# Input stage of a delta-rule layer: scans, decay projection, gathers, beta and averages in another order

## The chip, the cores and the metric

The kernel is one program on one core of a Trainium2 chip. Its engines work from queues of their own: TensorE (PE, matrix products and transposes), VectorE (DVE), ScalarE (ACT), GpSimd (POOL) and SyncE (SP, which issues transfers). They wait for one another through semaphores. The metric is the device time in microseconds (us) of the whole program.

## The reference, cut to what matters

Two layers run over 4096 tokens of width 256: causal linear attention and a mixture of eight experts (top two), then the delta-rule layer and a recurrent output stage. The change lies in the input part of the delta-rule layer. What it must compute:

```python
def short_conv(x, w):                 # 4 taps over the tokens
    ...
q = silu(short_conv(hidden_states @ Wq, conv_q))
k = silu(short_conv(hidden_states @ Wk, conv_k))
v = silu(short_conv(hidden_states @ Wv, conv_v))
mix_inp = silu(short_conv(hidden_states @ Wmix, conv_mix))
q = silu(q)
k = silu(k)
beta = jax.nn.sigmoid(hidden_states @ Wb)
gamma = jax.nn.sigmoid(hidden_states @ Wdec)
# ema_rule, for each head:
s = gt[..., None] * s + (1.0 - gt[..., None]) * vt
# delta rule: q and k to unit length, then k_beta @ k^T in chunks of 32, strictly lower part, its inverse
mix = jax.nn.sigmoid(mix_inp + mix_bias)
```

`hidden_states` is the layer-normed residual, to which the two chosen experts' rows have just been added.

## The kernel before

`build` calls `first_layer` (attention and experts), `delta_inputs` (the change is in it alone), `delta_rule` and `gated_output`. Between them all engines meet, so what `delta_inputs` gives up at its end moves all that follows.

`delta_inputs` works on eight groups (`NG`) of 512 tokens, features on the partitions. Every engine runs the same software pipeline of ten steps: in step i it handles group i (`new`: expert rows added, statistics, normed `xn`), group u = i - 1 (`here`: projections, convolutions, scans) and group v = i - 2 (`tiles`: transposes to token rows, Gram matrices, norms). Nothing reorders work: each engine's queue is what `step` writes.

- **Projections (PE `use(n)`, ACT `use(n)`).** `use(0)` and `use(1)` transpose `xn` into `xT`. The other nine follow `ORDER`: 4 and 5 are the two 128-row blocks of v, 2 and 3 of k, 0 and 1 of q, `"s"` is the small rows (beta, decay, mix with their taps), and `"g0"`, `"g1"` spread the decay row over the partitions, which needs `"s"` copied out first (four copies, line 1334). Three PSUM banks `pp` go round: a product may start when ScalarE has emptied the bank of three before. A block takes two ScalarE copies (lines 1343 and 1346).
- **Convolutions (DVE `conv(b)`).** Three multiply-adds at line 1479 on each block, then ScalarE's `silu(b)`: once for 4 and 5, twice for the others. The silus of 0 and 1 stand in ScalarE's next step.
- **Average (scans).** ScalarE puts tanh of g0 and g1 in `dec_t` (line 1339); GpSimd rescales it to `dec` (line 1294); VectorE makes the input (line 1515) and runs two scans (line 1521) that carry on from the previous group. `rows(...)`, in steps 5 to 8 only, computes rows of the first inverses (lines 1094 and 1097); SyncE sends them (line 1082) in step 9.
- **Token rows (PE, ACT `tokens(n)`).** Six transposes in two PSUM banks: n = 0, 3 of k, 1, 4 of v, 2, 5 of the averages. SyncE stores a pair of tiles after its three.
- **Norms.** ScalarE squares, PE `sums()` adds them up (line 1627), VectorE adds epsilon (`ss`, line 1529), forms scales and `l32` (line 1541), GpSimd takes powers (`root`, line 1301). Beta and mix come from `small_rows()` through ScalarE's tanh and silu; line 1498 (`sm_m`) feeds the second tanh (line 1413), which feeds lines 1508 and 1509.
- **GpSimd** besides gathers the expert rows of group i + 1 (line 1258, eight transfers, in two lots of four), and makes `rstd` (line 1283).

## Time and profile before

| | |
|---|---|
| time, median of 3 runs (lowest, highest) | 1425.54 us (1422.87, 1429.32) |
| the profiled execution: its time, its span | 1430.96 us, 1429.3 us |
| busy: PE, DVE, ACT, POOL | 89%, 58%, 32%, 35% of the span |
| `delta_inputs`, from its first gather to the next stage's start | 610 to 913 us |
| steps 2 to 4 of it (VectorE's) | 663.37 to 759.80 us |
| steps 5 to 7 | 759.80 to 856.06 us |
| mean granted TensorE clock | 0.919 |

The profiled execution is 5.4 us (0.4%) above the median of the runs; changes are summed against its rows and then taken off either. A row of a timeline reads: start, length, engine, line, operation, output <- inputs, shapes, count, and in brackets how long the engine stood idle before it and what released it. "PEclk" is the share of TensorE's full clock that was granted.

### The profile page before, as it was taken

The numbers are of one execution on the slowest core, as the hardware profiler recorded it, in microseconds if no ns is written. First come the engines' busy times: TensorE is split into PE (matmuls) and PEld (weight loads), VectorE is DVE, ScalarE is ACT, GpSimd is POOL, SyncE is SP. The second block draws the span as 40 slices with busy tenths as digits, with TensorE's granted clock in tenths as the row PEclk, the third lists the DMA queues.
The fourth block names the chain that finished last, engine by engine and source line by source line (L and its number), as shares of the span: only waits on it lengthen the run. The fifth ranks groups of instructions, "written<-read, shape, count | busy, mean of one in ns | idle before, by whom it ended". The sixth has DMA issues, their size and how long they took to land. (4 is left out here: it accounts for less than half of the span.)

```text
span 1429.3 us, 36337 instructions
## 1 busy us (share of the span) xinstructions
PE 1274.9 (89%) x12853; PEld 951.0 (67%) x12854; DVE 822.0 (58%) x1882; ACT 463.4 (32%) x1085; POOL 497.4 (35%) x711
## 2 busy tenths in 40 slices
PE   6999999899999999927889787498999999889997
PEld 5888888767777777614555454387888888646564
DVE  5778888633222222238789887357566666435443
ACT  1211112132222222217667776112222222123332
POOL 3334666414511111064665642223343444210000
PEclk9999999989999999968878888559999999779999
DMA  9999910112321111121454433712643335000001
GB/s 313 351 369 341 330 44 35 36 51 100 118 64 59 59 59 59 52 77 52 141 142 128 123 89 94 195 50 74 111 108 95 95 94 149 7 1 30 30 22 37
DMA packets 219962, 156.60 MB, mean 110 GB/s; under 512 B 111744, under 2 KB 201344, under 8 KB 219840
## 3 DMA queue, kind: packets, MB, share of 16 engines
q1 hardware_dynamic: 210528, 129.51, 30.9%
q0 software_dynamic: 9312, 25.44, 5.3%
q8 instruction: 80, 1.31, 0.4%
q14 instruction: 42, 0.34, 0.1%
HBM read 64.47 MB, written 90.44 MB: 108 GB/s over the span
## 5 line engine op out<-in xcount | busy, mean ns | idle before, releaser
L945 PE MATMUL ps_sc<-w,a_qeo 128*128 x568 | 183.3, 466 | 0.0
L753 DVE TENSOR_TENSOR a_stm<-a_vpad,ps_sc 128x352 f32<-128x352 f32 x71 | 37.0, 521 | 177.3 <-ACT a_vpad L517 156.6
L945 PEld LDWEIGHTS ps_sc<-w,a_qeo 128*128 128x128 f32 x568 | 104.1, 193 | 46.5 <-issue 2.5
L423 POOL DMA_DIRECT2D x_slots<-a_stm x66 | 36.5, 552 | 226.1 <-issue 226.1
L1583 PE MATMUL d_pp<-d_xT,d_w_p 128*128 128x512 f32 x192 | 110.3, 721 | 1.1 <-ACT d_xT L1328 1.1
L1479 DVE SCALAR_TENSOR_TENSOR d_cout<-d_cin,d_taps,d_cout 128x512 f32<-128x512 f32 x144 | 106.2, 747 | 6.4 <-ACT d_cout L1346 3.0
L915 PE MATMUL ps_kv<-w,a_stm 128*128 x426 | 105.7, 384 | 1.2 <-DVE a_stm L746 1.2
L915 PEld LDWEIGHTS ps_kv<-w,a_stm 128*128 128x128 f32 x426 | 79.3, 190 | 30.2 <-issue 12.7
L2326 PE MATMUL g_pp<-g_xT,g_w_g 128*128 128x512 f32 x192 | 89.3, 604 | 8.3 <-ACT g_xT L2217 8.3
L1258 POOL DMA_INDIRECT got<-x_slots,d_idx x64 | 74.0, 1156 | 18.7 <-issue 16.1
L517 ACT ACTIVATE a_vpad<-ps_sc 128x352 f32<-128x352 f32 x71 | 33.0, 464 | 140.1 <-PE ps_sc L945 140.1
L711 DVE TENSOR_TENSOR a_stm<-ps_sc,causal 128x2048 f32<-128x2048 f32 x32 | 73.0, 2282 | 1.7 <-PE ps_sc L854 1.3
L1583 PEld LDWEIGHTS d_pp<-d_xT,d_w_p 128*128 128x128 f32 x192 | 41.7, 232 | 45.8 <-issue 41.7
L415 POOL DMA_INDIRECT x_slots<-xn_res,slots x64 | 65.3, 1020 | 15.1 <-issue 14.8
L746 DVE COPY a_stm<-ps_t 128x384 f32<-128x384 f32 x71 | 39.6, 557 | 47.7 <-PE ps_t L924 47.4
L1824 POOL TENSOR_SCALAR u_ms<-u_ss 128x4 f32<-128x4 f32 x32 | 6.2, 195 | 173.1 <-DVE u_ss L1936 173.1
L890 PE MATMUL ps_qk<-a_xnT,w_qk 128*128 128x128 f32 x512 | 66.1, 283 | 0.0
L2326 PEld LDWEIGHTS g_pp<-g_xT,g_w_g 128*128 128x128 f32 x192 | 36.5, 193 | 44.2 <-issue 32.9
L890 PEld LDWEIGHTS ps_qk<-a_xnT,w_qk 128*128 128x128 f32 x512 | 61.3, 196 | 0.0
L2260 DVE TENSOR_TENSOR g_z<-g_py,g_b_o 128x256 f32<-128x256 f32 x32 | 13.6, 425 | 77.0 <-PE g_py L2341 77.0
L2063 PE MATMUL u_bank_g<-u_qkT 64*128 64x128 f32 x512 | 41.8, 308 | 17.3 <-DMA u_kve<-rec 17.3
L1876 ACT ACTIVATE u_GU<-u_bank_g 64x256 f32<-64x256 f32 x32 | 12.1, 378 | 134.9 <-PE u_bank_g L2063 134.9
(275 smaller groups left out, 2839.8 us busy)
## 6 DMA issues: line engine op xcount, KB each, us to landing
x_slots<-a_zeros SPq DMA_DIRECT2D x32, 1024.0 KB, 10.9
rec<-d_kve SPq DMA_DIRECT2D x32, 384.0 KB, 2.9
u_kve<-rec SPq DMA_DIRECT2D x32, 384.0 KB, 3.5
a_qeo<-x_slots SPq DMA_DIRECT2D x71, 128.0 KB
x_slots<-a_stm POOLq DMA_DIRECT2D x66, 128.0 KB
rec<-d_act_out SPq DMA_DIRECT2D x32, 256.0 KB
u_qkT<-rec SPq DMA_DIRECT2D x32, 256.0 KB, 3.1
w<-in_w SPq DMA_DIRECT2D x4, 1408.0 KB, 13.9
```

What stands on the lines that cost most here:

```text
L415: pool.indirect_dma_start(out=x_slots, out_offset=bass.IndirectOffsetOnAxis(ap=slots[:, choice, t:t + 1], axis=0), in_=xn2_res[:, t, :], i ...
L711: dve.tensor_tensor(stm[:, :, :], ps_sc[:, :].rearrange("p (h q) -> p h q", h=16), causal[:, :].unsqueeze(1).broadcast_to([P, 16, P]), ALU ...
L746: dve.tensor_copy(e_hT[:, q], ps_h[:, 0:3 * P].rearrange("p (b t) -> p b t", b=3)).then_inc(ht_out, 1)
L753: dve.tensor_tensor(e_h[:, q, 0:HID], e_gate[:, q, :], ps_3[q], ALU.mult).then_inc(h_out, 1)
L890: mm = pe.matmul(ps_qk[:, b * P:(b + 1) * P], w_qk[:, k, b * P:(b + 1) * P], xnT[:, q, k, :], start=(k == 0), stop=(k == KD - 1))
L915: mm = pe.matmul(ps_y, e_hT[:, q, b, :], w2[:, b, bass.ds(e_out, 1), :], start=(b == 0), stop=(b == 2))
L945: mm = pe.matmul(ps, e_xT[:, q, k, :], w13[:, s, k, bass.ds(e_hidden, 1), :], start=(k == 0), stop=(k == KD - 1))
L1258: pool.indirect_dma_start(out=got[:, q, j, s, :], out_offset=None, in_=x_slots, in_offset=bass.IndirectOffsetOnAxis(ap=idx[:, q, s, j:j + ...
L1479: dve.scalar_tensor_tensor(out=cout[:, b, :], in0=x[:, c:c + GW], scalar=taps[:, b, c:c + 1], in1=cout[:, b, :], op0=ALU.mult, op1=ALU.add)\
L1583: mm = pe.matmul(bank[:, :], lhs, xT[:, k, :], start=(k == 0), stop=(k == KD - 1))
L2063: mm = pe.matmul(b_g[:, e, z, n, :], qkT[rows, gs, 2 + n, :], qkT[rows, gs, what + n, :], start=True, stop=True)
L2326: mm = pe.matmul(bank[:, :], w_g[:, k, b // 2, (b % 2) * P:(b % 2 + 1) * P], xT[:, q, k, :], start=(k == 0), stop=(k == KD - 1))
```

## The change

Only orders change; every operation and its size stay.

- VectorE: the decay input and the two scans (with `rows`, where there are any) go from between mix and block 2's convolution to the end of the step. The three beta instructions go from behind block 5's convolution to ahead of block 4's (the fourth block, counted from 0). The convolution of block 3 moves ahead of the norms' scales.
- `ORDER` becomes 4, 5, 2, 3, "s", 0, 1, "g0", "g1".
- `tokens` run in the order 0, 1, 3, 4, 2, 5 (`TOK`): both averages last. TensorE's `sums()` moves ahead of `"s"`. SyncE waits accordingly and stores both pairs later.
- GpSimd: the second lot of gathers goes ahead of the rescale to `dec`, and that rescale also behind `root` and its two copies.
- ScalarE: `silu(2)` and `silu(3)` go between the last three `use`s, `silu(4)` ahead of `"s"`.

VectorE, one steady step before, from the end of block 5's convolution on (`d_ema` rows are the two scans, `d_cout` rows the convolutions, `d_l` is `l32`):

```order
L1496 TENSOR_SCALAR d_beta<-d_sm_t 128x16
L1497 TENSOR_SCALAR d_beta<-d_sm_t 128x16
L1498 TENSOR_TENSOR d_sm_m<-d_sm_m,d_mix_b 128x16
L1504 TENSOR_SCALAR d_xn<-x_res,d_mom,d_rstd 128x256 x4
L1508 TENSOR_SCALAR d_rest<-d_sm_t 128x16
L1509 TENSOR_SCALAR small<-d_sm_t 128x4x4
L1515 SCALAR_TENSOR_TENSOR d_dec_t<-d_dec_t,d_act_out 128x1024
L1521 SCALAR_TENSOR_TENSOR d_ema<-d_dec,d_ema,d_dec_t 128x512 x2
L1479 SCALAR_TENSOR_TENSOR d_cout<-d_cin,d_taps,d_cout 128x512 x3
L1529 TENSOR_SCALAR d_ss<-d_ps_s 128x32
```

The same stretch now:

```order
L1509 TENSOR_SCALAR d_xn<-x_res,d_mom,d_rstd 128x256 x4
L1513 TENSOR_SCALAR d_rest<-d_sm_t 128x16
L1514 TENSOR_SCALAR small<-d_sm_t 128x4x4
L1484 SCALAR_TENSOR_TENSOR d_cout<-d_cin,d_taps,d_cout 128x512 x6
L1521 TENSOR_SCALAR d_ss<-d_ps_s 128x32
L1524 RECIPROCAL d_over<-d_ss 128x16
L1527 TENSOR_TENSOR small<-d_beta,d_over 128x4x4
L1528 TENSOR_TENSOR small<-d_beta,d_over 128x4x4
L1533 TENSOR_TENSOR d_l<-d_ps_g,small 128x8x32 x2
L1484 SCALAR_TENSOR_TENSOR d_cout<-d_cin,d_taps,d_cout 128x512 x6
L1544 SCALAR_TENSOR_TENSOR d_dec_t<-d_dec_t,d_act_out 128x1024
L1550 SCALAR_TENSOR_TENSOR d_ema<-d_dec,d_ema,d_dec_t 128x512 x2
```

The scans moved past four convolutions and the scales; the beta rows have gone ahead of this stretch.

GpSimd, one steady step before:

```order
L1254 COPY d_idx<-slots 128x8
L1258 DMA got<-x_slots,d_idx 128x256 x4
L1281 TENSOR_SCALAR d_shifted<-d_mom 128x4
L1283 TENSOR_TENSOR d_rstd<-d_shifted,d_power 128x4
L1294 TENSOR_SCALAR d_dec<-d_dec_t 128x1024
L1258 DMA got<-x_slots,d_idx 128x256 x4
L1301 TENSOR_TENSOR d_root<-d_ss,d_power 128x32
```

and now:

```order
L1283 TENSOR_SCALAR d_shifted<-d_mom 128x4
L1285 TENSOR_TENSOR d_rstd<-d_shifted,d_power 128x4
L1260 DMA got<-x_slots,d_idx 128x256 x4
L1299 TENSOR_TENSOR d_root<-d_ss,d_power 128x32
L1302 TENSOR_TENSOR small<-d_root,d_rest 128x4x4
L1303 COPY small<-d_root 128x4x4
L1307 TENSOR_SCALAR d_dec<-d_dec_t 128x1024
L1311 COPY d_cin<-d_cin 128x6x3
```

The rescale to `d_dec` now stands behind four gathers and the powers.

TensorE, the middle of one steady step now (`d_w_s` is the "s" projection, `d_sel_q` the sums, `d_sel_d` g0 and g1); before, "s" stood ahead of the sums by seven rows:

```order
L1624 MATMUL d_ps_g<-d_act_out 32x32 x64
L1588 MATMUL d_pp<-d_xT,d_w_p 128x512 x2
L1605 MATMUL d_ps_tok<-d_ident,d_act_out 128x128 x4
L1588 MATMUL d_pp<-d_xT,d_w_p 128x512 x2
L1633 MATMUL d_ps_s<-d_sel_q,d_sq 128x8 x16
L1588 MATMUL d_pp<-d_xT,d_w_s 128x512 x2
L1605 MATMUL d_ps_tok<-d_ident,d_ema 128x128 x4
L1588 MATMUL d_pp<-d_xT,d_w_p 128x512 x2
L1605 MATMUL d_ps_tok<-d_ident,d_ema 128x128 x4
L1588 MATMUL d_pp<-d_xT,d_w_p 128x512 x2
L1579 MATMUL d_pp<-d_s_rows,d_sel_d 128x512 x2
```

The averages' transposes, the decay's products and "s" are all late in the step.

The core of the diff:

```diff
-        ORDER = [4, 5, "s", 2, "g0", "g1", 3, 0, 1]
+        ORDER = [4, 5, 2, 3, "s", 0, 1, "g0", "g1"]
...
+        TOK = [0, 1, 3, 4, 2, 5]
+        TOKS = len(TOK)
...
-                        sp.wait_ge(tok_out, 6 * u + 3 * pair + 3)
+                        sp.wait_ge(tok_out, TOKS * u + TOK.index(3 * pair + 2) + 1)
...
-                if has(u, NG):
-                    pool.wait_ge(p_out, USES * u + after_use("g1"))
-                    wait(pool, ema_done, 2 * u)
-                    pool.tensor_scalar(dec[:, :, :], dec_t[:, :, :], 0.5, 0.5, ALU.mult, ALU.add).then_inc(dec_done, 1)
                 if has(i + 1, NG):
                     gather(i + 1, 1 - par, (2, 3))
...
                     pool.tensor_copy(small[:, tiles, 4 * H:5 * H], root[:, :, 1, :]).then_inc(kept_done, 1)
+                if has(u, NG):
+                    pool.wait_ge(p_out, USES * u + after_use("g1"))
+                    wait(pool, ema_done, 2 * u)
+                    pool.tensor_scalar(dec[:, :, :], dec_t[:, :, :], 0.5, 0.5, ALU.mult, ALU.add).then_inc(dec_done, 1)
...
                     add_experts(i, par, 1)
+                if tiles:
+                    dve.wait_ge(sm_out, v + 1)
...
                 if here:
                     conv(4)
...
-                if i in EARLY_ROWS_AT:
-                    rows(*EARLY_ROWS_AT[i])
-                if here:
-                    dve.wait_ge(dec_done, u + 1)
...
                 if here:
                     conv(2)
+                    conv(3)
...
                 if here:
-                    conv(3)
                     conv(0)
                     conv(1)
+                if i in EARLY_ROWS_AT:
+                    rows(*EARLY_ROWS_AT[i])
+                if here:
+                    dve.wait_ge(dec_done, u + 1)
...
```

## Rows read from the trace of the kernel before

**Rows 1.** Stretches: start:end, us, busy by engine (count), PEclk, DMA share, GB/s
```profile
663.37:759.80 96.43, 84.42 (x697) 51.01 (x696) 77.17 (x157) 68.11 (x129) 56.98 (x47) 0.85 0.45 126
695.17:727.43 32.26, 28.10 (x234) 16.71 (x233) 25.69 (x54) 22.70 (x43) 19.63 (x17) 0.87 0.48 129
759.80:856.06 96.26, 81.57 (x698) 49.18 (x697) 86.60 (x181) 68.48 (x130) 48.77 (x39) 0.87 0.43 118
```

**Rows 2.** Timeline of VectorE: one row of step 1, then step 3
```profile
650.92 1.23 DVE L1515 SCALAR_TENSOR_TENSOR d_dec_t<-d_dec_t,d_act_out 128x1024 f32<-128x1024 f32 x1 [0.94 <-POOL d_dec L1294]
...
703.63 0.18 DVE L1461 BATCH_NORM_AGGREGATE d_mom<-d_stats 128x2 f32<-128x6 f32 x1
...
706.19 1.39 DVE L1504 TENSOR_SCALAR d_xn<-x_res,d_mom,d_rstd 128x256 f32<-128x256 f32 x4
709.33 0.17 DVE L1508 TENSOR_SCALAR d_rest<-d_sm_t 128x16 f32<-128x16 f32 x1 [1.75 <-ACT d_sm_t L1413]
...
713.45 1.23 DVE L1515 SCALAR_TENSOR_TENSOR d_dec_t<-d_dec_t,d_act_out 128x1024 f32<-128x1024 f32 x1 [3.87 <-POOL d_dec L1294]
...
719.33 0.18 DVE L1529 TENSOR_SCALAR d_ss<-d_ps_s 128x32 f32<-128x32 f32 x1
...
720.72 6.79 DVE L1479 SCALAR_TENSOR_TENSOR d_cout<-d_cin,d_taps,d_cout 128x512 f32<-128x512 f32 x9
```

**Rows 3.** Timeline of GpSimd, step 3
```profile
704.63 1.53 POOL L1283 TENSOR_TENSOR d_rstd<-d_shifted,d_power 128x4 f32<-128x4 f32 x1
...
712.37 1.05 POOL L1294 TENSOR_SCALAR d_dec<-d_dec_t 128x1024 f32<-128x1024 f32 x1 [6.21 <-ACT d_dec_t L1339]
...
720.27 5.47 POOL L1301 TENSOR_TENSOR d_root<-d_ss,d_power 128x32 f32<-128x32 f32 x1
```

**Rows 4.** The page's costliest groups: busy, mean ns of one, idle before
```profile
L1479 DVE SCALAR_TENSOR_TENSOR d_cout<-d_cin,d_taps,d_cout 128x512 f32<-128x512 f32 x144 | 106.2, 747 | 6.4 <-ACT d_cout L1346 3.0
...
L1258 POOL DMA_INDIRECT got<-x_slots,d_idx x64 | 74.0, 1156 | 18.7 <-issue 16.1
```

**Rows 5.** Timeline of TensorE, step 3
```profile
693.22 3.59 PE L1583 MATMUL d_pp<-d_xT,d_w_p 128*128 128x512 f32 x4
...
703.81 1.88 PE L1583 MATMUL d_pp<-d_xT,d_w_p 128*128 128x512 f32 x4
705.53 0.60 PE L1599 MATMUL d_ps_tok<-d_ident,d_act_out 128*128 128x128 f32 x4
...
709.60 3.63 PE L1627 MATMUL d_ps_s<-d_sel_q,d_sq 128*128 128x8 f32 x32
```

**Rows 6.** Stretch in which that first product ran, columns as in rows 1
```profile
692.00:697.00 5.00, 4.84 (x12) 2.48 (x13) 4.79 (x10) 3.10 (x9) 4.33 (x7) 0.55 0.32 37
```

**Rows 7.** Timeline of ScalarE, step 3
```profile
703.57 2.76 ACT L1334 ACTIVATE d_s_rows<-d_pp,d_tap_rows 32x512 f32<-32x512 f32 x4 [1.30 <-PE d_pp L1583]
...
708.03 0.59 ACT L1343 ACTIVATE d_cin<-d_pp 128x512 f32<-128x512 f32 x1
...
709.08 0.23 ACT L1413 ACTIVATE d_sm_t<-d_sm_m 128x16 f32<-128x16 f32 x1
...
719.57 0.63 ACT L1360 ACTIVATE d_act_out<-d_cout 128x512 f32<-128x512 f32 x1
...
720.77 0.58 ACT L1343 ACTIVATE d_cin<-d_pp 128x512 f32<-128x512 f32 x1
```

**Rows 8.** Stretches of the inverse rows, steps 5 to 8: us, VectorE busy, PEclk
```profile
774.14:778.59 4.45, 4.00 (x17) 0.98 0.41 158
806.85:810.05 3.20, 3.02 (x8) 1.00 0.18 71
838.15:841.13 2.98, 2.87 (x6) 1.00 0.12 45
869.15:876.62 7.47, 7.26 (x9) 0.83 0.65 210
```

**Rows 9.** Timeline of SyncE's queue, step 9
```profile
888.78 10.04 SPq L1082 DMA_DIRECT2D t_mat<-d_t_early  x12
```

More of the change, by code:

```diff
@@ L1355, in silu @@
                         wait(act, qk_sent, 64 * (u - 1))
-                    wait(act, tok_done, 6 * (u - 1))
+                    wait(act, tok_done, TOKS * (u - 1))
                     wait(act, g_done, u - 1)
@@ L1368, in tokens @@
                     pair, what = n // 3, n % 3
-                    act.wait_ge(tok_done, 6 * v + n + 1)
+                    at = TOKS * v + TOK.index(n)
+                    act.wait_ge(tok_done, at + 1)
                     if what == 0:
                         wait(act, kve_sent[pair], 32 * v)
-                    act.activation(kve[:, 2 * pair:2 * pair + 2, what, :], ps_tok[n % 2][:, :].rearrange("p (j c) -> p j c", j=2),
+                    act.activation(kve[:, 2 * pair:2 * pair + 2, what, :], ps_tok[at % 2][:, :].rearrange("p (j c) -> p j c", j=2),
                                    ACT.Copy, scale=-0.5 if what == 2 else 1.0).then_inc(tok_out, 1)
@@ L1422, in step @@
                     use(7)
+                if tiles:
+                    tokens(5)
+                if here:
                     use(8)
+                    silu(u, q, 2)
                     use(9)
-                    silu(u, q, 2)
+                    silu(u, q, 3)
                     use(10)
-                    silu(u, q, 3)
             pipelined(act, NG, DEPTH, step, singly=NG)
@@ L1485, in step @@
                     add_experts(i, par, 1)
+                if tiles:
+                    dve.wait_ge(sm_out, v + 1)
+                    wait(dve, kept_done, v)
+                    dve.tensor_scalar(beta[:, 0], sm_t[:, 0], 0.5, 0.5, ALU.mult, ALU.add).then_inc(beta_done, 1)
+                    dve.tensor_scalar(beta[:, 1], sm_t[:, 0], -0.5, -0.5, ALU.mult, ALU.add).then_inc(beta_done, 1)
+                    dve.tensor_tensor(sm_m[:, :, :], sm_m[:, :, :], mix_b[:, :].unsqueeze(1).broadcast_to([P, GROUP, H]),
+                                      ALU.add).then_inc(sm_add, 1)
                 if here:
@@ L1492, in step @@
                     conv(5)
-                if tiles:
-                    dve.wait_ge(sm_out, v + 1)
-                    wait(dve, kept_done, v)
-                    dve.tensor_scalar(beta[:, 0], sm_t[:, 0], 0.5, 0.5, ALU.mult, ALU.add).then_inc(beta_done, 1)
-                    dve.tensor_scalar(beta[:, 1], sm_t[:, 0], -0.5, -0.5, ALU.mult, ALU.add).then_inc(beta_done, 1)
-                    dve.tensor_tensor(sm_m[:, :, :], sm_m[:, :, :], mix_b[:, :].unsqueeze(1).broadcast_to([P, GROUP, H]),
-                                      ALU.add).then_inc(sm_add, 1)
                 if new:
@@ L1509, in step @@
                     dve.tensor_scalar(sm[:, :, H:2 * H], sm_t[:, 1], 0.5, 0.5, ALU.mult, ALU.add).then_inc(mix_done, 1)
-                if i in EARLY_ROWS_AT:
-                    rows(*EARLY_ROWS_AT[i])
-                if here:
-                    dve.wait_ge(dec_done, u + 1)
-                    dve.wait_ge(silu_done, 6 * u + 2)
-                    dve.scalar_tensor_tensor(out=dec_t[:, :, :], in0=dec_t[:, :, :], scalar=1.0, in1=act_out[:, q, 4:6, :],
-                                             op0=ALU.subtract, op1=ALU.mult).then_inc(inp_done, 1)
-                    dve.wait_ge(inp_done, u + 1)
-                    wait(dve, tok_done, 6 * (u - 1))
-                    wait(dve, ema_done, 2 * u)
-                    for b in range(2):
-                        dve.tensor_tensor_scan(ema[:, q, b, :], dec[:, b, :], dec_t[:, b, :],
-                                               0.0 if u == 0 else ema[:, 1 - q, b, GW - 1:GW], ALU.mult, ALU.add)\
-                           .then_inc(ema_done, 1)
                 if here:
                     conv(2)
+                    conv(3)
                 if tiles:
@@ L1544, in step @@
                 if here:
-                    conv(3)
                     conv(0)
                     conv(1)
+                if i in EARLY_ROWS_AT:
+                    rows(*EARLY_ROWS_AT[i])
+                if here:
+                    dve.wait_ge(dec_done, u + 1)
+                    dve.wait_ge(silu_done, 6 * u + 2)
+                    dve.scalar_tensor_tensor(out=dec_t[:, :, :], in0=dec_t[:, :, :], scalar=1.0, in1=act_out[:, q, 4:6, :],
+                                             op0=ALU.subtract, op1=ALU.mult).then_inc(inp_done, 1)
+                    dve.wait_ge(inp_done, u + 1)
+                    wait(dve, tok_done, TOKS * (u - 1))
+                    wait(dve, ema_done, 2 * u)
+                    for b in range(2):
+                        dve.tensor_tensor_scan(ema[:, q, b, :], dec[:, b, :], dec_t[:, b, :],
+                                               0.0 if u == 0 else ema[:, 1 - q, b, GW - 1:GW], ALU.mult, ALU.add)\
+                           .then_inc(ema_done, 1)
             pipelined(dve, NG, DEPTH, step, singly=NG)
@@ L1592, in tokens @@
                         pe.wait_ge(ema_done, 2 * (v + 1))
-                    wait(pe, tok_out, 6 * v + n - 1)
+                    turn = TOKS * v + TOK.index(n)
+                    wait(pe, tok_out, turn - 1)
                     for j in range(2):
@@ L1652, in step @@
                 if tiles:
-                    tokens(4)
+                    sums()
                 if here:
@@ L1660, in step @@
                 if tiles:
-                    sums()
+                    tokens(5)
                 if here:
```

15 lines of the change are left out of this document (7 added, 8 removed).

## The prediction
> **What bounds the kernel now.** I read the stretches first, then one steady step engine by engine. Steps 2 to 4 of the input stage take 96.43 us, 32.1 each, and step 3 takes 32.26 [rows 1]. VectorE is busy for 25.7 of that, TensorE for 28.1, ScalarE for 22.7, so none is full. Where VectorE stands still is the timeline's to show: 1.75 us before the mix rows, for ScalarE's second tanh, and 3.87 us before the decay input, for GpSimd's rescale [rows 2]. Without these two a step of VectorE is 32.26 - 5.62 = 26.64 us, small gaps included. The rescale had itself waited 6.21 us for ScalarE's tanh of g1 [rows 3]. That wait closes a circle: VectorE's convolution of block 3, its silu, ScalarE's and TensorE's next step down to g1, the rescale, decay input, scans, convolution of block 2, scales, block 3 again. TensorE's waits lie on the same circle; one is followed by a product that takes 3.59 us where the same product takes 1.88 [rows 5], in a stretch whose granted clock is 0.55, near the lower level of 1.2 GHz [rows 6].
>
> **VectorE: scans last, block 3 early, beta early.** The scans feed only the averages' transposes, which now stand late in the next step. So the circle through the scans is cut, and both waits lose their cause: the tanh has its input 4 us earlier relative to ScalarE, and the decay input is asked for last. What is late next, by the same rows:
>
> 1. `xn` needs `rstd`, which ends 706.16, 2.35 us after the last statistics row ends [rows 2, 3]. Block 5's convolution takes 2.23 of that; the beta rows that hid the remainder are gone from there. Wait 0.24.
>
> 2. The decay input needs the rescale, which stands behind `root`. `root` can start some 0.3 us after `ss` and takes 5.47 [rows 2, 3]; its two copies take about 0.5 and the rescale 1.05, so the input can start 7.3 us after `ss`. VectorE meanwhile does the scales, 1.39 (719.33 to 720.72), and two convolutions, 2 x 2.24 (6.71 for three) [rows 2]: 5.9. Wait 1.4 to 1.5, where there are no inverse rows.
>
> VectorE's own period is thus 26.64 + 0.24 + 1.5 = **28.4 us**.
>
> **GpSimd: gathers ahead of the rescale.** Four gathers start right after `rstd`, about 11.3 us into VectorE's step, and `ss` comes at 17.3 (8.8 for additions, beta and block 4; 2.2; 0.24; 1.4 for `xn`; 0.2; 4.5). A gather takes 1.16 on average and the idle time before it 0.29 (18.7 over 64) [rows 4], four of them 5.8, until 17.1, so `root` is not held up; gathers of twice that length bound it at 5.6 us. The tiles are wanted only a step later.
>
> **TensorE and ScalarE: their own circle.** ScalarE's copies of `xT` start the first product, TensorE goes through to "s", and ScalarE works from there to the next `xT`. First piece: from 693.22 to 705.53 TensorE does five projections (one slow), three transposes and the Gram matrices, the set that now precedes the sums: 12.3 us. The sums take 3.63 and "s" 1.88 [rows 5]. ScalarE's piece: four row copies 2.8; two pairs of copies at 1.05 (708.03 to 709.08); two double silus at 1.20 (719.57 to 720.77); five single operations at about half a pair, 2.5; `xT` 1.05; hand-overs 0.15 [rows 7]. Together 11.0. The circle is 12.3 + 3.6 + 1.9 + 11.0 = **28.8 us**, 27.1 if the first product ran at full clock, and 30.5 if "s", right behind the narrow sums, also ran at the low one. It is 0.4 above VectorE's, with some 4 us of slack before block 0 or g1 holds VectorE, but less in step 2, where ScalarE starts late. For steps 2 to 4 I take 28.8.
>
> SyncE stores both pairs later, then q and k, then `l32`; nothing waits for these before the next step, so I price this at nothing while the step stays over 25 us. The cover is the step itself.
>
> **The sum**, against the profiled execution:
>
> - Step 1 has no norms; its wait of 0.94 for the rescale [rows 2] goes, since four convolutions now cover it: 0.9.
> - Steps 2 to 4: 96.4 - 3 x 28.8 = 10.0 [rows 1].
> - Steps 5 to 7: the inverse rows (4.45, 3.20, 2.98) [rows 8] now lie in VectorE's wait for the rescale and cover it wholly, but before they covered most of the 3.87 too. 3 x 26.88 + 10.63 = 91.3 against 96.3 [rows 1]: 5.0.
> - Step 8, and the end. The stage's end is SyncE's: the early inverses go out from 888.78, 10.04 us of issuing [rows 9], then the last group's stores; this tail of 24 us to 913 stays. Before, it started 32.7 after step 8 began (856.06). Now it starts when the inverse rows are ready. Step 8 has no additions and no `xn`, so VectorE waits for TensorE's circle: block 3 of step 7 ends 17.3 into a step of 29.9, the first product starts 3.0 later (silu, g1, `xT`), "s" ends 17.8 after that, and block 0 is out of its bank after another 4.9, at 43.0, that is 13.1 into step 8. Two convolutions, 4.5, and the rows, 7.5 [rows 8]: 25.1. I take SyncE to be free by then; if not, its lateness adds to this one for one. Gain 7.6.
>
> 0.9 + 10.0 + 5.0 + 7.6 = 23.5 us. The profiled 1430.96 becomes 1407.5; the median of the runs, 1425.54, becomes **1402.0 us**.
>
> **A rule of the skill.** `root` ran from 720.27 to 725.74 beside the convolutions of 720.72 to 727.43 [rows 2, 3]; these took 754 ns each, against 747 over all 144 [rows 4]. So neither engine stood still for the other. The Trainium skill (SBUF — State Buffer, "Who interferes with whom") says that a VectorE instruction with two SBUF inputs contends with a GpSimd instruction that reads SBUF, and that the later one blocks wholly. By that rule these rows could not stand as they do; the result that it would give here is rival D.
>
> **The rivals.**
>
> A. *ScalarE and TensorE become the bound.* "s" behind the sums runs at the low clock each time. Circle 30.5: steps 2 to 4 take 91.5, steps 5 to 7 about 92.3, the tail starts at 26.8. Gain 0.9 + 4.9 + 4.0 + 5.9 = 15.7: 1409.8. For it speaks that TensorE already falls to the low clock once a step [rows 6]; against it, that its waits get shorter. 12 in 100.
>
> B. *The waits of TensorE shrink below what lowers its clock, and GpSimd's powers cost less than I think.* Steps 2 to 4 at 26.9, the tail at 23.4: 0.9 + 15.7 + 5.0 + 9.3 = 30.9: 1394.6. The powers' 5.47 stands in the rows, so this asks for much. 8 in 100.
>
> C. *Slower: TensorE at the low clock throughout.* The new order leaves it several waits of 0.5 to 2 us between g0 and the first product. If it never got back to full clock, the circle would gain 1.7 for each of three more projections, 1.9 for "s", and 2 for transposes and Gram matrices: 28.8 + 9 = 38. Six steps at 38 against 32.1 are +35: 1461. It decides from 32.1 us, that is two projections more at the low clock in every step. Against it: 0.87 was granted on average, with TensorE idle for 4 us of step 3 [rows 1]. 4 in 100.
>
> D. *No change: powers and convolutions exclude each other.* Blocks 0 and 1 would begin only when `root` has ended, 4.1 us late; less the wait of 1.5 that vanishes, 2.6 in each of steps 2 to 4, and 4.1 in each of 5 to 7, 20 us in all: 1422. Rows 2 to 4 speak against it. 2 in 100.
>
> E. *No change: the gain is given back.* Gathers or stores hold the new order up (`root` late by 5.6 us a step, gathers of twice the length, in all six steps: 34, less about 12 that inverse rows cover, 22): 1424. 6 in 100.
>
> The forecast itself, 18 to 28 us of gain, has 68 in 100.
>
> **How the numbers follow.** Range: A and B inside, with their bounds: 1394 to 1413. Outside lie C, D and E, 12 in 100, and the fringes. What a measurement of this kernel can tell from no change is about 0.5%, 7 us. Faster by over that: forecast, A, B, 0.88; within it: D and E, 0.07; slower: C and something unforeseen, 0.05.
>
> **What would show it.** VectorE's row before the mix loses its wait; the decay input stands behind four convolutions with a wait near 1.5 for GpSimd in steps 2 to 4 and none in 5 to 8; `xn` waits 0.2 for `rstd`. Steps 2 to 4 take 28.4 to 29, step 5 31.3, and SyncE's early inverses start about 25 us into step 8. `delta_rule` and what follows keep their lengths. It is wrong if VectorE waits more than 3 us for anything in a steady step, if "s" takes over 3 us (A), or if the convolutions beside `root` grow over 0.8 us (D).

## The result, and the profile after

The changed kernel takes 1422.38 us (median of 20 runs, 1417.73 to 1430.82); the kernel before, run beside it, 1430.76 us (20 runs). The ratio is 0.9952, 95% interval 0.9935 to 0.9969: 6.9 us faster by the ratio, 8.4 by the two medians, where 23.5 were forecast. The time lies outside the range of 1394 to 1413. (The forecast started from 1425.54, the median of three runs of the kernel before; the median of 20 is 5.2 us higher, so by that start it would have read 1407.3.) The profiled execution took 1430.82 us (span 1429.2), the longest of its 20, so its stages are compared one by one and not by the whole. On a second chip the changed kernel's profiled execution (`a_again`, 1420.99 us) is the median one; it is used below to see what is steady.

The stage now ends (first row of the next one) at 906.68 instead of 913.11 us: 6.4 us earlier. By VectorE's steps the same stretches as in [rows 1] are, with PE, PEld, DVE, ACT and POOL busy, then PEclk, DMA share and GB/s:

```profile
662.91:756.22 93.31, 83.07 (x692) 49.43 (x691) 77.66 (x158) 65.44 (x126) 59.21 (x46) 0.88 0.45 128
692.57:724.92 32.35, 27.80 (x233) 16.58 (x232) 25.91 (x54) 22.50 (x43) 19.91 (x16) 0.89 0.45 127
756.22:853.07 96.85, 89.95 (x786) 53.53 (x785) 87.57 (x182) 70.70 (x136) 51.50 (x39) 0.85 0.44 118
698.00:702.00 4.00, 4.00 (x26) 1.76 (x14) 3.79 (x10) 0.01 (x1) 0.47 (x1) 0.50 0.00 0
```

| part | before | after | gain | forecast |
|---|---|---|---|---|
| up to step 2 | 663.37 | 662.91 | 0.5 | 0.9 |
| steps 2 to 4 | 96.43 | 93.31 | 3.1 | 10.0 |
| steps 5 to 7 | 96.26 | 96.85 | -0.6 | 5.0 |
| step 8 to the early inverses' issue | 32.7 | 30.7 | 2.0 | 7.6 |
| from there to the stage's end | 24.3 | 22.9 | 1.4 | 0 |
| sum | | | 6.4 | 23.5 |

Of steps 5 to 7 it is step 5 alone that missed: 36.02 us where 31.3 were forecast; steps 6 and 7 took 30.88 and 29.95, against 30.1 and 29.9.

Step 3 alone did not get shorter at all: 32.35 against 32.26. VectorE's timeline of it, against [rows 2]:

```profile
688.93 1.23 DVE L1544 SCALAR_TENSOR_TENSOR d_dec_t<-d_dec_t,d_act_out 128x1024 f32<-128x1024 f32 x1 [1.43 <-POOL d_dec L1307]
...
703.82 1.47 DVE L1509 TENSOR_SCALAR d_xn<-x_res,d_mom,d_rstd 128x256 f32<-128x256 f32 x4 [0.16 <-POOL d_rstd L1285]
706.14 0.32 DVE L1513 TENSOR_SCALAR d_rest<-d_sm_t 128x16 f32<-128x16 f32 x1 [0.86 <-ACT d_sm_t L1416]
...
715.25 4.57 DVE L1484 SCALAR_TENSOR_TENSOR d_cout<-d_cin,d_taps,d_cout 128x512 f32<-128x512 f32 x6 [3.01 <-ACT d_cout L1348]
721.28 1.22 DVE L1544 SCALAR_TENSOR_TENSOR d_dec_t<-d_dec_t,d_act_out 128x1024 f32<-128x1024 f32 x1 [1.46 <-POOL d_dec L1307]
```

The forecast waits are there, 0.16 and 1.4 us; the one before the mix rows did not go wholly, 0.86 is left. The old 3.87 before the decay input is gone. In its place stands one that the forecast did not have: 3.01 us before block 0's convolution, for ScalarE's copy of block 0 out of TensorE's bank. In step 5 it is 4.93, ahead of the inverse rows, so that these cover nothing, and in step 8 it is 5.97:

```profile
779.87 4.56 DVE L1484 SCALAR_TENSOR_TENSOR d_cout<-d_cin,d_taps,d_cout 128x512 f32<-128x512 f32 x6 [4.93 <-ACT d_cout L1348]
...
871.63 4.57 DVE L1484 SCALAR_TENSOR_TENSOR d_cout<-d_cin,d_taps,d_cout 128x512 f32<-128x512 f32 x6 [5.97 <-ACT d_cout L1348]
```

TensorE's timeline says why block 0 is late:

```profile
693.34 0.56 PE L1624 MATMUL d_ps_g<-d_act_out 64*32 64x32 f32 x41
694.21 0.25 PE L1624 MATMUL d_ps_g<-d_act_out 64*32 64x32 f32 x3 [0.31 <-issue]
694.95 0.25 PE L1624 MATMUL d_ps_g<-d_act_out 64*32 64x32 f32 x3 [0.49 <-issue]
695.71 0.27 PE L1624 MATMUL d_ps_g<-d_act_out 64*32 64x32 f32 x3 [0.51 <-issue]
696.45 0.21 PE L1624 MATMUL d_ps_g<-d_act_out 64*32 64x32 f32 x1 [0.47 <-issue]
697.17 1.08 PE L1624 MATMUL d_ps_g<-d_act_out 64*32 64x32 f32 x77 [0.52 <-issue]
698.18 3.78 PE L1588 MATMUL d_pp<-d_xT,d_w_p 128*128 128x512 f32 x4
...
704.63 3.63 PE L1633 MATMUL d_ps_s<-d_sel_q,d_sq 128*128 128x8 f32 x32
708.12 1.96 PE L1588 MATMUL d_pp<-d_xT,d_w_s 128*128 128x512 f32 x4
```

The Gram products (L1624) stop five times for about 0.5 us with nothing awaited ("issue"), and the projection behind them takes 3.78 us instead of the 1.98 that it takes in the steps with one stop or none; the clock granted from 698 to 702 is 0.50, the lower level (last stretch above). ScalarE waits for that projection, 5.71 us, and its row copies of "s" start at 710.12:

```profile
702.00 0.60 ACT L1345 ACTIVATE d_cin<-d_pp 128x512 f32<-128x512 f32 x1 [5.71 <-PE d_pp L1588]
...
710.12 2.76 ACT L1336 ACTIVATE d_s_rows<-d_pp,d_tap_rows 32x512 f32<-32x512 f32 x4 [3.49 <-PE d_pp L1588]
...
720.01 1.08 ACT L1330 ACTIVATE d_xT<-d_pp 128x512 f32<-128x512 f32 x2
```

GpSimd issues the first lot of gathers from 690.49 to 696.35, and all stops but the last lie in that time. `root` ran beside convolutions at its old length [rows 3]:

```profile
690.49 1.86 POOL L1260 DMA_INDIRECT got<-x_slots,d_idx  x1 [0.28 <-POOL d_idx L1256]
692.65 1.19 POOL L1260 DMA_INDIRECT got<-x_slots,d_idx  x1 [0.30 <-issue]
694.15 0.95 POOL L1260 DMA_INDIRECT got<-x_slots,d_idx  x1 [0.30 <-issue]
695.41 0.94 POOL L1260 DMA_INDIRECT got<-x_slots,d_idx  x1 [0.30 <-issue]
...
711.04 5.47 POOL L1299 TENSOR_TENSOR d_root<-d_ss,d_power 128x32 f32<-128x32 f32 x1 [1.60 <-DVE d_ss L1521]
```

Before, the Gram products of this step ran from 699.33 with a single stop of 0.47: the last of the first four gathers had been issued at 699.01, so only the end of the lot met them. After, they begin behind the second of the four. In `a_again` the stops add up to less: 1.03, 1.01 and 1.56 us in steps 3 to 5, and only the projection behind the last was slow (3.49). The circle of ScalarE and TensorE, from one copy of `xT` to the next, is 31.7, 32.4, 31.3, 33.3 and 31.4 us in steps 1 to 5, where the forecast had 28.8 (in `a_again` 32.0, 31.6, 31.6, 33.0 and 28.3). SyncE's early inverses, to [rows 9], and the page's group, to [rows 4]:

```profile
883.80 9.47 SPq L1082 DMA_DIRECT2D t_mat<-d_t_early  x12
```
```profile
L1484 DVE SCALAR_TENSOR_TENSOR d_cout<-d_cin,d_taps,d_cout 128x512 f32<-128x512 f32 x144 | 107.2, 755 | 21.7 <-ACT d_cout L1348 18.3
```

**The theory** that the experiments test: the circle of ScalarE and TensorE sets the steps, not VectorE; it is some 3 us longer than forecast because (a) gathers stop the Gram products and leave the next projection at the low clock, and (b) "s", right behind the narrow sums, often runs at the low clock too (3.76, 1.96, 1.96, 3.76, 3.41, 2.98, 3.76 us in the seven groups with sums ahead of it). Rivals: VectorE itself is the bound; the low clock behind the sums alone is the cause; GpSimd's late rescale is (`e6_pool_old` bears on this one).

### The profile page after: what moved, and what is told of

It is laid out like the page before. It is cut to its first block and busy times, and to the rows that moved or that the text cites. A ratio compares the mean times of both kernels' runs of the same rounds, so it can differ in the third digit from the quotient of the medians.

```text
span 1429.2 us, 36337 instructions
## 1 busy us (share of the span) xinstructions
PE 1291.0 (90%) x12853; PEld 961.6 (67%) x12854; DVE 824.2 (58%) x1882; ACT 461.1 (32%) x1085; POOL 500.5 (35%) x711
## 5 line engine op out<-in xcount | busy, mean ns | idle before, releaser
L1484 DVE SCALAR_TENSOR_TENSOR d_cout<-d_cin,d_taps,d_cout 128x512 f32<-128x512 f32 x144 | 107.2, 755 | 21.7 <-ACT d_cout L1348 18.3
L1588 PE MATMUL d_pp<-d_xT,d_w_p 128*128 128x512 f32 x192 | 106.7, 688 | 4.9 <-ACT d_xT L1330 4.9
L915 PEld LDWEIGHTS ps_kv<-w,a_stm 128*128 128x128 f32 x426 | 79.3, 190 | 30.2 <-issue 12.7
L2332 PEld LDWEIGHTS g_pp<-g_xT,g_w_g 128*128 128x128 f32 x192 | 36.5, 193 | 44.2 <-issue 32.9
L1588 PEld LDWEIGHTS d_pp<-d_xT,d_w_p 128*128 128x128 f32 x192 | 38.7, 222 | 39.4 <-issue 31.7
## 6 DMA issues: line engine op xcount, KB each, us to landing
w<-in_w SPq DMA_DIRECT2D x4, 1408.0 KB, 13.7
```

Of the source, the lines that this page charges most:

```text
L915: mm = pe.matmul(ps_y, e_hT[:, q, b, :], w2[:, b, bass.ds(e_out, 1), :], start=(b == 0), stop=(b == 2))
L1484: dve.scalar_tensor_tensor(out=cout[:, b, :], in0=x[:, c:c + GW], scalar=taps[:, b, c:c + 1], in1=cout[:, b, :], op0=ALU.mult, op1=ALU.add)\
L1588: mm = pe.matmul(bank[:, :], lhs, xT[:, k, :], start=(k == 0), stop=(k == KD - 1))
L2332: mm = pe.matmul(bank[:, :], w_g[:, k, b // 2, (b % 2) * P:(b % 2 + 1) * P], xT[:, q, k, :], start=(k == 0), stop=(k == KD - 1))
```

## The experiments

The ratios are to the kernel before, run on the same chip, with 95% intervals. The changed kernel itself stood at 0.9952 above, and on a second chip (`a_again`) at 0.9930.

**Is VectorE the bound?** One of each three convolution instructions works on 8 columns instead of 512, so a part of each convolution is left out.

```diff
+                        w = 8 if c == 1 else GW
-                        dve.scalar_tensor_tensor(out=cout[:, b, :], in0=x[:, c:c + GW], ...
+                        dve.scalar_tensor_tensor(out=cout[:, b, 0:w], in0=x[:, c:c + w], ...
```

> The changed kernel with the second multiply-add of each convolution cut from 512 to 8 columns, so that part of the convolution is left out; VectorE loses some 4 us of work in each of steps 1 to 8. Theory 1 (the circle of ScalarE and TensorE sets the steps, 31.5 us each): VectorE's idle time grows by what was cut, and the whole gets at most 5 us faster, from step 8 and the first steps. Rival (VectorE with GpSimd's powers still sets the steps): 4 us a step in seven steps, about 28 us faster than the changed kernel.

Measured: 1416.86 us, 0.9884 (0.9862 to 0.9907). The circles of steps 1 to 5 are 28.6, 32.9, 31.6, 32.4 and 31.7. Only the first fell, by 3.1, and there TensorE had less to do: the sums took 3.74 instead of 4.44 and "s" 1.96 instead of 3.76. On the page, the convolutions work 25 us less than in the changed kernel (107.2) and VectorE waits 11 us more before them (21.7); the timeline of step 3 has 5.23 where 3.01 stood:

```profile
L1485 DVE SCALAR_TENSOR_TENSOR d_cout<-d_cin,d_taps,d_cout 128x512 f32<-128x512 f32 x144 | 82.0, 579 | 32.7 <-ACT d_cout L1348 29.3
```
```profile
709.40 3.51 DVE L1485 SCALAR_TENSOR_TENSOR d_cout<-d_cin,d_taps,d_cout 128x512 f32<-128x512 f32 x6 [5.23 <-ACT d_cout L1348]
715.42 1.23 DVE L1545 SCALAR_TENSOR_TENSOR d_dec_t<-d_dec_t,d_act_out 128x1024 f32<-128x1024 f32 x1 [2.51 <-POOL d_dec L1307]
```

Of 25 us of work the time got back some 7 to 10 (0.9884 against 0.9930 and 0.9952): more than the 5 that the theory allowed. Step 1, in which VectorE has no norms to do and this circle is not yet closed, gave 3.2 (25.64 to 22.47) and step 5 gave 1.9; steps 2 to 4 took 92.4 against 93.3, though VectorE had some 3 us less to do in each. In the steady steps VectorE is not the bound.

**Is it the sums?** First, `sums()` goes behind block 0's projection, so that "s" follows a projection:

```diff
-                if tiles:
-                    sums()
...
                     use(8)
+                if tiles:
+                    sums()
+                if here:
```

> The changed kernel with one edit: TensorE's sums go from ahead of the small rows' projection to behind the last q projection, off the circle. Theory 1: the circle loses the 3.6 to 5 us of the sums and gains about 1.2 where g0 comes late, so steps go from 31.5 to about 28.5 to 29 and the whole gets 12 to 20 us faster than the changed kernel. Rival 1 (what is lost is TensorE's low clock and stalls, wherever the sums stand): within 5 us of the changed kernel. Rival 2 (VectorE sets the steps): no change, or slower, since the scales come later.

Measured: 1410.29 us, 0.9838 (0.9804 to 0.9872), inside what was expected. "s" takes 1.88 in every step, steps 2 to 4 are 28.22, 28.25 and 28.34, the waits before block 0 are gone, and those for the rescale stay:

```profile
712.14 1.23 DVE L1544 SCALAR_TENSOR_TENSOR d_dec_t<-d_dec_t,d_act_out 128x1024 f32<-128x1024 f32 x1 [1.42 <-POOL d_dec L1307]
```

So VectorE's own period, forecast at 28.4, is right, and it rules once the circle is shorter. The Gram products still stop, 4.7 us in all, and one projection behind them takes 3.78. The product that now stands behind the sums (g0) is slow in six of seven steps, 2.81 to 3.76, so the low clock moved with the sums and did not go. Second, only k's squares are summed (q's sums are left out), which halves the narrow products and leaves them in place:

```diff
-                        for b in range(4):
+                        for b in (2, 3):
```

> The changed kernel with the sums of q's squares left out, so that the sums take 8 products and not 16, and q's norms are not formed. Theory 1: 1.8 us off the circle in each of steps 2 to 7 and some more in step 8, 9 to 13 us faster than the changed kernel. Rival (VectorE sets the steps): no change.

Measured: 1405.75 us, 0.9799 (0.9770 to 0.9828), more than expected. Each "s" now takes 1.96:

```profile
703.07 1.95 PE L1633 MATMUL d_ps_s<-d_sel_q,d_sq 128*128 128x8 f32 x16
704.88 1.96 PE L1588 MATMUL d_pp<-d_xT,d_w_s 128*128 128x512 f32 x4
```

Half of the sums are 1.8 us a step; the low clock behind them costs up to 1.8 more. The stops are all there, 5.6 us in steps 3 to 5, with two slow projections behind them (3.58, 3.65), and steps 2 to 4 took 86.2 us all the same.

**Is it the gathers?** The first lot waits until TensorE has finished the step's Gram products. Nothing else changes; `a_again` is the changed kernel once more, on the same chip.

```diff
+                    wait(pool, g_done, i - 1)
                     gather(i + 1, 1 - par, (0, 1))
```

> The changed kernel with one wait added: GpSimd starts the first lot of gathers only when TensorE has ended the Gram matrices of that step. In steps 3 and 4 these products stood still 4 to 5 times for half a microsecond with nothing to wait for, while those gathers ran. Theory (gathers hold up the feeding of TensorE's many small products): the gaps go, 2 us off the circle in steps 3 and 4, 3 to 5 us faster than the changed kernel in all. Rival (the gaps have another cause, the stores for one): gaps stay at 4 to 7 us in all, time within 2 us, or slower because rstd comes later.

> The changed kernel once more, on the chip of the runs beside it: a ratio to the kernel before of 0.993 to 0.997, and the same picture, SyncE's and TensorE's waits in the same places, with TensorE's circle at 29 to 33 us a step.

Measured: 1408.25 us, 0.9822 (0.9776 to 0.9868), against 1420.99, 0.9930 (0.9907 to 0.9953) without the wait. Steps 2 to 4 of VectorE are 29.44, 29.03 and 28.31 us; the circles 31.5, 28.1, 28.4, 27.8, 31.3, 28.5. Expected were 3 to 5 us against the changed kernel; it is 12.7. The trace of `a_again` has 3.6 us of stops and 1.5 for a slow projection to give back, 5.1, and its circles of steps 1 to 5 shrink by 9.3 in all; where the rest comes from is not shown. The gain over the kernel before (1432.18 on that chip), 24 us, is the one forecast for the change, and the parts agree: steps 2 to 4 take 86.8 (forecast 86.4), and the early inverses go out 25.8 us into step 8 (forecast 25.1). GpSimd and TensorE in step 3:

```profile
694.38 0.62 POOL L1256 COPY d_idx<-slots 128x8 uint32<-128x8 uint32 x1 [7.07 <-PE d_ps_g L1625]
695.28 1.39 POOL L1260 DMA_INDIRECT got<-x_slots,d_idx  x1 [0.28 <-POOL d_idx L1256]
```
```profile
693.01 1.29 PE L1625 MATMUL d_ps_g<-d_act_out 64*32 64x32 f32 x128
694.24 1.98 PE L1589 MATMUL d_pp<-d_xT,d_w_p 128*128 128x512 f32 x4
696.06 0.60 PE L1606 MATMUL d_ps_tok<-d_ident,d_act_out 128*128 128x128 f32 x4
696.49 1.88 PE L1589 MATMUL d_pp<-d_xT,d_w_p 128*128 128x512 f32 x4
698.52 3.74 PE L1634 MATMUL d_ps_s<-d_sel_q,d_sq 128*128 128x8 f32 x32
702.12 1.96 PE L1589 MATMUL d_pp<-d_xT,d_w_s 128*128 128x512 f32 x4
```

No stop in any step, and no projection behind the Gram products over 1.99 us. Of the change's own stretch, Gram products plus the next projection, 8.4 us (693.34 to 701.75) became 3.05 (693.01 to 696.06); in `a_again`, without the wait, it was 4.7. Here "s" still ran at the low clock in five of seven steps (3.76, 2.68, 2.92, 3.76, 2.62), and the steps were short all the same, but for the circles of 31.5 and 31.3 in which the sums took 5.04 and 4.82 and "s" 3.76. So neither (a) alone (`e2_sums_late`, `e5_sums_short`) nor (b) alone (this run) holds the change back by much; it takes both, and either one's cure frees it.

**Does the wait help any order?** The same line in the kernel before.

```diff
+                    wait(pool, g_done, i - 1)
                     gather(i + 1, 1 - par, (0, 1))
```

> The kernel before, with one wait added: the first lot of gathers of a step starts only when TensorE has finished the Gram products. Theory: the wait is worth what the gathers take from the Gram products. In the trace of before the products stand still for only about 1 us in all six steps, against 3.6 to 4.7 in the changed kernel, and its steps are set by VectorE's circle through the rescale; so little is to be had: ratio to before 0.995 to 1.003. Rival: the wait helps any order (its cause is in the gathers themselves and the low clock behind them): ratio 0.985 or below, as the changed kernel gained 0.011 by it. Second rival: the gathers, started later, delay the rescale that stands between their two lots, and so the scans: 1.005 or above.

Measured: 1428.21 us, 0.9974 (0.9952 to 0.9996). As the theory had it: the loss became large only in the new order. Before, the Gram products stopped for 1 us in all, so there was little to give back. The run does not say how it would be without a price of its own: GpSimd now makes `rstd` late, VectorE waits 1.3 to 2.1 us for it in steps 2 to 6, and its wait for the rescale falls from 3.87 to between 2.6 and 3.1.

**Do the cures add up?** The changed kernel with the wait and with the sums behind block 0's projection.

> The changed kernel with both cures: first gathers behind the Gram products, and the sums behind the last q projection. Theory: either cure alone already brings the circle of ScalarE and TensorE below VectorE's own period (28.3 to 29), so they don't add up: steps 2 to 4 of 28.2 to 28.4, ratio to before 0.978 to 0.984 (e7 had 0.982, e2 0.984). Rival: each removes its own loss on the path, and they add: 0.972 or below. What would show the theory: the decay input still waits 1.4 us for the rescale in steps 2 to 4, and nothing else of VectorE waits more than 1 us there.

Measured: 1405.67 us, 0.9815 (0.9787 to 0.9843). Steps 28.27, 28.30, 28.33; the only VectorE waits over 0.2 us in them are 1.42, 1.42 and 1.39 for the rescale. They don't add: VectorE, with its wait for the rescale, is the bound.

**Then VectorE's waits.** As the last, with GpSimd's rescale ahead of `root`, and in step 8 the inverse rows ahead of blocks 0 and 1:

```diff
+                if has(u, NG):
+                    ... (rescale to dec)
                 if tiles:
                     ... (root and its copies)
-                if has(u, NG):
-                    ... (rescale to dec)
...
+                if i == NG:
+                    rows(*EARLY_ROWS_AT[i])
                 if here:
                     conv(0)
                     conv(1)
```

> As the kernel with both cures, and GpSimd's rescale between the second gathers and the powers, and in step 8 the inverse rows ahead of blocks 0 and 1. Theory: VectorE is the bound there, so its wait of 1.4 us for the rescale goes in steps 2 to 4 (4 us), and the last early inverses go out about 4 us earlier: 4 to 8 us less than the kernel with both cures, ratio to before 0.973 to 0.979, steps 2 to 4 of 26.9 to 27.3. Rival: g1 is late, so the rescale holds up the powers, and the wait moves to the scales or the next step: no gain, 0.980 to 0.985, with waits for GpSimd's powers of 2 us or more.

Measured: 1403.18 us, 0.9805 (0.9777 to 0.9833). The stage ends at 885.1 instead of 889.8, the wait for the rescale is gone, and the steps are 27.4, where 26.9 to 27.3 were expected. The whole is 2.5 us under the kernel with both cures, where 4 to 8 were expected, and the intervals can't tell it from nothing. Where the rest went, VectorE and GpSimd in step 4 say:

```profile
736.93 5.21 DVE L1485 SCALAR_TENSOR_TENSOR d_cout<-d_cin,d_taps,d_cout 128x512 f32<-128x512 f32 x6
```
```profile
737.43 1.15 POOL L1299 TENSOR_SCALAR d_dec<-d_dec_t 128x1024 f32<-128x1024 f32 x1 [1.87 <-ACT d_dec_t L1342]
738.56 5.88 POOL L1304 TENSOR_TENSOR d_root<-d_ss,d_power 128x32 f32<-128x32 f32 x1
```

The same six convolutions took 4.55 with both cures alone. The one that starts at 737.71, inside the rescale, takes 1.41 us instead of 0.75, and so does one in each of steps 2 to 7:

```profile
737.71 1.41 DVE L1485 SCALAR_TENSOR_TENSOR d_cout<-d_cin,d_taps,d_cout 128x512 f32<-128x512 f32 x1
```

28.3 - 1.4 + 0.66 = 27.6, within 0.2 of what was measured.

**The rows elsewhere.** The inverse rows ahead of blocks 0 and 1, in steps 5 to 8 as the only edit; and then in step 8 alone, together with the late sums (`e9_best`):

```diff
+                if i in EARLY_ROWS_AT:
+                    rows(*EARLY_ROWS_AT[i])
                 if here:
                     conv(0)
                     conv(1)
-                if i in EARLY_ROWS_AT:
-                    rows(*EARLY_ROWS_AT[i])
```

> The changed kernel with the inverse rows of steps 5 to 8 ahead of the convolutions of blocks 0 and 1 and not behind them, where VectorE waits for the q projection (4.9 us in step 5, 6.0 in step 8). Theory 1 (that wait is what the rows can fill): steps 5 and 8 lose 4.5 and 6 us, the early inverses go out earlier, 6 to 10 us faster in all than the changed kernel. Rival (the circle of ScalarE and TensorE sets all steps, rows or not): 0 to 3 us, from the tail alone.

> The changed kernel with the sums behind the last q projection, as in the earlier run, and in step 8 alone the inverse rows ahead of blocks 0 and 1. Theory: steps as in that run (28.3 in steps 2 to 4), and the early inverses go out 4.5 us sooner, 3 to 5 us faster than that run, ratio to before about 0.980. Rival (SyncE's own stores set the tail): no faster than that run.

Measured: `e3_rows_mid` 1422.02 us, 0.9912 (0.9881 to 0.9943). The wait before block 0 in step 5 falls from 4.93 to 0.41, and one of 1.5 for the rescale appears in steps 5 to 7. That is 3 to 6 us under the changed kernel by the two ratios, where 6 to 10 were expected, and the intervals overlap. `e9_best` 1408.99 us, 0.9853 (0.9804 to 0.9903), no better than with the sums late alone, 0.9838, where 0.980 was expected. The rows did get ready earlier: the early inverses went out at 862.08 against 862.20, although the Gram products had stopped for 2.95 us in step 4 and made that step 2.8 longer. But the stage did not end with them. It ended 11.74 us behind VectorE's last `ss`, which waits for TensorE's sums (6.14 us here, 7.93 with the sums late alone), and it ends 11.73 or 11.74 us behind that row in the kernel before, in `e2_sums_late`, `e8_scans_only`, `b_gather_wait`, `e10_wait_sums` and `e11_dec_early` too. In the changed kernel it is 17.07, and SyncE issues almost without a break from the early inverses on.

**Parts alone.** The kernel before with only VectorE's scans and rows moved to the end of its step:

```diff
-                if i in EARLY_ROWS_AT:
-                    rows(*EARLY_ROWS_AT[i])
-                if here:
-                    ... (decay input and the two scans)
...
                     conv(1)
+                if i in EARLY_ROWS_AT:
+                    rows(*EARLY_ROWS_AT[i])
+                if here:
+                    ... (decay input and the two scans)
```

> The kernel before with one part of the change: decay input and scans (and the inverse rows) at the end of VectorE's step; all other orders as before. Theory 1 (the scans leave the circle, TensorE's order then sets it): TensorE's 26.8 us from the first projection to the last, then about 3.5 on ScalarE, so 30.3 us a step against 32.1: 5 to 12 us faster than before, as much as the whole change brought. Rival (the gain came from the other moves, the scans alone only move the wait): within 3 us of before.

Measured: 1445.91 us, 1.0092 (1.0060 to 1.0125): slower, and outside what was expected. With the old order of projections block 3 comes from TensorE behind the narrow sums (4.61 us in this step). ScalarE waits for it, and VectorE, which has no scans to fill the time, waits until ScalarE has copied it (683.29 + 0.68):

```profile
682.80 0.60 ACT L1343 ACTIVATE d_cin<-d_pp 128x512 f32<-128x512 f32 x1 [4.70 <-PE d_pp L1583]
683.29 0.68 ACT L1346 ACTIVATE d_cout<-d_pp,d_taps 128x512 f32<-128x512 f32 x1
```
```profile
684.01 6.92 DVE L1479 SCALAR_TENSOR_TENSOR d_cout<-d_cin,d_taps,d_cout 128x512 f32<-128x512 f32 x9 [3.35 <-issue]
```

And the Gram products stop for 8.3 us in all, one time in step 8, where no gather is issued any more:

```profile
868.17 0.44 PE L1618 MATMUL d_ps_g<-d_act_out 64*32 64x32 f32 x24 [1.73 <-issue]
```

The scans' move alone costs 13 us. That the new `ORDER` is what makes it pay is argued from these rows; no run has the two alone. The other part, the changed kernel with GpSimd's order as before:

```diff
+                if has(u, NG):
+                    ... (rescale to dec)
                 if has(i + 1, NG):
                     gather(i + 1, 1 - par, (2, 3))
...
-                if has(u, NG):
-                    ... (rescale to dec)
```

> The changed kernel with only GpSimd's order as before: the rescale ahead of the second gathers and of the powers. Theory: the loss lies in the first gathers, which stand where they did, and in the circle of ScalarE and TensorE; so GpSimd's order behind them changes little: ratio to before 0.990 to 0.997, as the changed kernel (0.993 to 0.995), with 0.5 us gaps in the Gram products as there. Rival: the later rescale and its wait of 1.4 us in steps 2 to 4 were what held the changed kernel back: 0.988 or below. Second rival: with g1 last in the order, a rescale ahead of the powers makes these late, and the gather of the next group too: 1.000 or above.

Measured: 1427.53 us, 0.9966 (0.9943 to 0.9989). The number is in the theory's span, the reason is not: the gathers stand behind the rescale, which waits for g1, now the last projection, and VectorE waits for the expert rows:

```profile
700.35 1.00 DVE L1460 SCALAR_TENSOR_TENSOR x_res<-got,gates,x_res 128x256 f32<-128x256 f32 x2 [5.23 <-DMA got<-x_slots,d_idx]
```

The same wait is 2.90, 4.18 and 3.07 in the steps beside it. So the change needs the gathers ahead of the rescale, by the trace; the whole time, 0.9966, is not clearly apart from the changed kernel's. The rival, that the late rescale held the change back, asked for 0.988 or below. It wasn't seen, but the new waits could hide a gain; the cleaner sign is `e11_dec_early`, in which the rescale's wait went and a steady step became 0.9 us shorter.

## Why the prediction was wrong

- **Step 1, scans cut out of the circle: right.** The wait of 3.87 us went, and VectorE's own period was 28.2 to 28.3 in every kernel in which nothing else held it (forecast 28.4), with 0.16 for `xn` (0.24 forecast, though its own terms, 2.35 less 2.23, give 0.12) and 1.39 to 1.42 for the rescale (1.4 to 1.5).
- **The circle of ScalarE and TensorE, 28.8 us: this term failed.** Its ScalarE piece was right: from the row copies to the next `xT` 9.9 us in nearly every step, and with `xT`'s own 1.08 the forecast 11.0. TensorE's piece, 12.3 + 3.6 + 1.9, was too small. The 12.3 was read off a stretch of the kernel before (four projections in both orders, where the text counts five) in which the Gram products stopped once for 0.47; in step 3 after they stopped five times, 2.3 us, and the projection behind them took 1.8 more, while the first projection took 1.6 less. The sum took "s" at full clock and kept 30.5 for rival A; after, five of seven "s" took 2.98 to 3.76. By TensorE's and ScalarE's rows the circles of steps 1 to 5 split like this:

| | forecast | 1 | 2 | 3 | 4 | 5 |
|---|---|---|---|---|---|---|
| `xT` copy to the sums | 13.5 | 13.7 | 17.0 | 15.8 | 14.7 | 14.2 |
| sums and "s" | 5.5 | 8.1 | 5.4 | 5.6 | 8.7 | 7.2 |
| "s" to the next `xT` copy | 9.8 | 9.9 | 9.9 | 9.9 | 9.9 | 9.9 |
| circle | 28.8 | 31.7 | 32.4 | 31.3 | 33.3 | 31.4 |

  So the gathers, (a), made circles 2 and 3 long, and the sums with the low clock behind them, (b), circles 1, 4 and 5. In `e7_gather_wait`, where there were neither stops nor a slow "s" in circle 2, it is 28.1: the sum was right for the work as it had priced it.
- **"Some 4 us of slack before block 0 or g1 holds VectorE": wrong by the same amount**, and this is where the loss enters. Its own sign of being wrong, VectorE waiting over 3 us in a steady step, came (3.01). The wait stands before block 0 and so ahead of the inverse rows, which the forecast had counted as cover in steps 5 to 7 (5.0 forecast, -0.6 measured) and in step 8.
- **Gathers at nothing: right for GpSimd's queue** (`root` found its input last, 1.60 idle before it) **and wrong for TensorE.** The prediction asked only who waits behind the gathers on their own queue. The gather wait, one line, gave back 12.7 us (1420.99 to 1408.25), and with it the change has its forecast gain.
- **"s" at full clock: the price was taken from a projection that doesn't follow the sums.** The 1.88 of [rows 5] is from 703.81. The projection behind the sums stood in the same trace and was slow there too, 3.29 us in step 3 and over 2.5 in four of seven steps; its stretch has a granted clock of 0.57, so 12 in 100 for rival A was too little:

```profile
713.09 7.09 PE L1583 MATMUL d_pp<-d_xT,d_w_p 128*128 128x512 f32 x12
```
```profile
713.09:716.38 3.29, 3.29 (x7) 1.49 (x7) 2.89 (x3) 0.00 (x0) 2.82 (x3) 0.57 1.00 308
```

- **Step 8: 7.6 forecast, 2.0 measured**, by the wait of 5.97; with the sums late the early inverses went out at 862.20 and with the gather wait at 865.77, against 883.80. The tail behind it shrank by 1.4, unforecast: "the stage's end is SyncE's" holds for the changed kernel (22.9 from the early inverses on), but in the kernel before the end hung on VectorE's last `ss` at 901.37, 11.73 us ahead of it, as in the runs named with `e9_best`.
- **Rival A** had the right place and sign, and half of the cause: 1409.8 forecast, with a circle of 30.5. **Rivals D and E**, at 1422 and 1424, name the measured 1422.38 by luck: no `root` was late, no gather took twice its length, and beside the kernel before the change gained 6.9 us, not the 3.5 and 1.5 that they stand for.
- **Rival D's** mechanism did not show beside `root`: 755 ns a convolution, `root` 5.47. The 8 ns over the kernel before are mostly one convolution of step 1, which took 1.53 us beside the rescale, so that six took 5.34 and not 4.56:

```profile
654.13 5.34 DVE L1484 SCALAR_TENSOR_TENSOR d_cout<-d_cin,d_taps,d_cout 128x512 f32<-128x512 f32 x6
```

  The Trainium skill (SBUF — State Buffer, "Who interferes with whom") says that the later of the two instructions blocks. Beside `root` the trace does not show that; beside the rescale of 128x1024 it does, in that step and in `e11_dec_early`, 1.41 us instead of 0.75, the end 0.5 us behind the rescale's; blocked to the last it would have ended 0.75 behind it.

The size of each share in the whole is not settled to the last microsecond: the stages behind this one took 516 to 525 us in single executions, whatever the kernel (516.2 before and 522.5 after in the two profiled ones, which eats the 6.4 us of this stage), and two cures that each suffice can't be given parts of a sum.

## What to carry to other kernels

When a wait is cut out of one circle, the next circle sets the step, and its slack has to be worked out with what it is exposed to in its new place, not read off as a sum of durations from the old one. Moving gathers, or moving what runs beside them, is priced on the other engines too, not on the gathers' own queue alone. A duration is taken from a row in the same neighbourhood: the price of a projection behind the sums stood in the trace, one row further down. And look where the next wait would stand: ahead of filler work it can't be filled by it.
